# Windowed attention on Trainium2: the turn of the older chunk goes in front of the scores, its copy in front of the row maximum

## What is computed

```python
q, k = rmsnorm(rope(x @ wq.T)), rmsnorm(rope(x @ wk.T)); v = x @ wv.T
mask = (cols <= rows) & (rows - cols <= WINDOW)          # WINDOW = 128
scores = einsum('bqgtd,bqgsd->bqgts', q, k) / sqrt(64)   # 16 heads of q, one k
attn = softmax(where(mask, scores, NEG))
out = einsum('bqgts,bqgsd->bqgtd', attn, v)
return h + reshape(out) @ wo.T
```

## Time and profile before

| | |
|---|---|
| median of 3 timed runs | 976.79 us (975.57, 976.79, 984.98) |
| the profiled execution | 969.34 us, of which the span is 967.1 us |
| busy over the span: PE, DVE, ACT, POOL | 747.3, 630.0, 443.2, 383.2 us |
| mean granted TensorE clock | 0.897 of full speed |
| the four `windowed` stages, from the first to the last row maximum of each | 97.3 to 166.6, 227.6 to 296.6, 360.1 to 429.4 and 490.3 to 558.2 us |

### The profile page before, as it was taken

The page is one execution under the profiler, slowest core; times in us unless marked ns, Lnnn a source line. Parts: engine busy times, 40 slices in busy tenths (PEclk is TensorE's granted clock), DMA queues, the critical chain, the costliest instruction groups (busy, mean ns, idle before and its releaser), DMA issues. The chain is left out here.

```text
span 967.1 us, 21086 instructions
## 1 busy us (share of the span) xinstructions
PE 747.3 (77%) x8204; PEld 482.5 (50%) x8204; DVE 630.0 (65%) x1210; ACT 443.2 (46%) x1389; POOL 383.2 (40%) x432
## 2 busy tenths in 40 slices
PE   5577999887998879998769989978899965302870
PEld 5232677434775326774257744864577732201650
DVE  0378788596886787876968847676677728500890
ACT  0022899234995228991369935213666610200210
POOL 0035466254663445662646622652000000074475
PEclk9999999998999889999979999988999977655875
DMA  8144000080000620000300000008000021014200
GB/s 287 59 174 83 2 3 2 21 238 2 3 2 1 210 49 1 4 2 1 84 2 3 2 2 1 2 1 111 2 2 2 2 78 43 1 52 102 50 20 13
DMA packets 59992, 41.60 MB, mean 43 GB/s; under 512 B 51744, under 2 KB 57340, under 8 KB 59108
## 3 DMA queue, kind: packets, MB, share of 16 engines
q1 hardware_dynamic: 57446, 33.03, 13.7%
q10 hardware_dynamic: 144, 4.19, 1.1%
q0 software_dynamic: 2304, 3.04, 1.0%
HBM read 25.44 MB, written 7.15 MB: 34 GB/s over the span
## 5 line engine op out<-in xcount | busy, mean ns | idle before, releaser
L770 ACT ACTIVATE work<-ps,small,rq 128x160 f32<-128x160 f32 x512 | 243.1, 487 | 54.2 <-DVE small L719 53.7
L749 POOL TENSOR_TENSOR work<-work,small 128x512 f32<-128x512 f32 x128 | 133.3, 1042 | 138.1 <-DVE small L733 138.1
L716 DVE TENSOR_REDUCE ps<-ps 128x4 f32<-128x640 f32 x128 | 106.5, 832 | 52.4 <-PE ps L639 52.1
L727 DVE COPY pT<-ps 128x640 f32<-128x640 f32 x128 | 105.4, 823 | 8.2 <-PE ps L652 7.9
L770 ACT ACTIVATION_READ_ACCUMULATOR work<-ps,small,rq 128x1 f32 x512 | 105.2, 206 | 0.0
L1441 POOL DMA_INDIRECT sent_rows<-big,xb x32 | 30.9, 966 | 182.4 <-DVEq L1393 173.0
L639 PE MATMUL ps<-kT,big 64*128 64x160 f32 x1024 | 102.6, 322 | 0.0
L269 PE MATMUL ps<-xT,s_proj_w 64*128 64x512 f32 x288 | 78.9, 661 | 21.5 <-DVE prod L581 13.2
L669 PE MATMUL ps<-pT,vwin 128*64 128x128 f32 x1024 | 84.2, 282 | 10.6 <-ACT big L758 2.4
L609 POOL TENSOR_TENSOR big<-prod 128x1024 f32<-128x1024 f32 x28 | 66.4, 2372 | 47.5 <-DVE prod L581 47.0
L639 PEld LDWEIGHTS ps<-kT,big 64*128 64x128 f32 x1024 | 80.3, 200 | 0.4
(11 more groups left out here) (275 smaller groups left out, 1361.2 us busy)
## 6 DMA issues: line engine op xcount, KB each, us to landing
xb<-in_x SPq DMA_DIRECT2D x3, 4096.0 KB, 12.7
xb<-in_x ACTq DMA_DIRECT2D x1, 4096.0 KB, 15.1
vrem<-hl SPq DMA_DIRECT2D x64, 64.0 KB, 2.2
sent_rows<-empty_row SPq DMA_DIRECT2D x8, 325.0 KB, 10.0
s_proj_w<-in_proj_w SPq DMA_DIRECT2D x1, 1536.0 KB, 6.5
big<-sent_rows SPq DMA_DIRECT2D x5, 264.0 KB, 5.1
big<-sent_rows SPq DMA_DIRECT2D x5, 256.0 KB, 4.6
xb<-in_ffn_w SPq DMA_DIRECT2D x1, 1028.0 KB, 4.9
```

Source lines behind the costliest of these rows:

```text
L716: ch.step(v.tensor_reduce(row_max(c), ps[:, s_banks(c), 0:2 * SPAN].rearrange("p e (h k) -> p e h k", h=2), X, ALU.max))
L727: v.tensor_copy(pT[:, c % 2, :].rearrange("p (q r t) -> p r q t", r=2, t=D), ps[:, 4:6, 0:(NQ + 1) * D].rearrange("p r (q t) -> p r q t", ...
L749: g.tensor_tensor(probs[:, c % 3, :, 0:P], probs[:, c % 3, :, 0:P], bc(small[:, c % 4, 3, :], P), ALU.mult)
L770: nc.scalar.activation(probs[:, c % 3, q, :], bank[2 * (c % 2) + e][:, SPAN * hh:SPAN * hh + SPAN], ACT.Exp, bias=small[:, c % 4, 1, q:q + ...
```

## The change

PE's loop body in `windowed` calls `turn(n - 3)` first and not between `scores(n)` and `values(n - 4)`. DVE's loop body does the copy of the turned rows (now in a small function, `keep_turned_rows`) ahead of the row maximum of chunk n and not behind its bias. The waits of each step are the same as before.

```diff
--- before.py
+++ after.py
@@ -671,6 +671,8 @@
                     ins.then_inc(S["pv_done"], 1)
 
                 for n in range(CHUNKS + 4):
+                    if 3 <= n < CHUNKS + 3:
+                        turn(n - 3)
                     if n < CHUNKS:
                         scores(n)
                     if n == 1 and b + 1 < IMAGES:
@@ -682,8 +684,6 @@
                         turn_halves(tokensT, 6, S["tokens_turned"])
                     if n == 4 and b + 1 < IMAGES:
                         pe.wait_ge(S["h_ready"], 1)
-                    if 3 <= n < CHUNKS + 3:
-                        turn(n - 3)
                     if n >= 4:
                         values(n - 4)
                 pe.wait_ge(S["oT_ready"], CHUNKS)
@@ -701,6 +701,14 @@
             @block.vector
             def _(v):
                 ch = Chain(v, S["dve_chain"])
+
+                def keep_turned_rows(c):
+                    v.wait_ge(S["transposed"], c + 1)
+                    if c >= 2:
+                        v.wait_ge(S["pv_done"], c - 1)
+                    v.tensor_copy(pT[:, c % 2, :].rearrange("p (q r t) -> p r q t", r=2, t=D),
+                                  ps[:, 4:6, 0:(NQ + 1) * D].rearrange("p r (q t) -> p r q t", t=D)).then_inc(
+                                      S["pT_ready"], 1)
 
                 for n in range(CHUNKS + 3):
                     c = n
@@ -711,6 +719,8 @@
                         v.wait_ge(S["tokens_turned"], 1)
                         v.tensor_copy(h_next.rearrange("p (w j) d -> p j w d", w=2),
                                       bank[6][:].rearrange("p (j w d) -> p j w d", w=2, d=D)).then_inc(S["h_ready"], 1)
+                    if n >= 3:
+                        keep_turned_rows(n - 3)
                     if c < CHUNKS:
                         v.wait_ge(S["scores_done"], c + 1)
                         ch.step(v.tensor_reduce(row_max(c),
@@ -719,14 +729,6 @@
                         v.scalar_tensor_tensor(out=small[:, c % 4, 1, :].rearrange("p (e h) -> p e h", e=2),
                                                in0=row_max(c), scalar=-1.0, in1=rq[:, c], op0=ALU.mult,
                                                op1=ALU.mult).then_inc(S["bias_ready"], 1)
-                    c = n - 3
-                    if c >= 0:
-                        v.wait_ge(S["transposed"], c + 1)
-                        if c >= 2:
-                            v.wait_ge(S["pv_done"], c - 1)
-                        v.tensor_copy(pT[:, c % 2, :].rearrange("p (q r t) -> p r q t", r=2, t=D),
-                                      ps[:, 4:6, 0:(NQ + 1) * D].rearrange("p r (q t) -> p r q t", t=D)).then_inc(
-                                          S["pT_ready"], 1)
                     c = n - 1
                     if 0 <= c < CHUNKS:
                         v.wait_ge(S["exp_done"], NQ * (c + 1))
```

## The result

The changed kernel takes 995.62 us (median of four runs, 993.63 to 996.94), the kernel before 976.18 (974.29 to 984.98): 1.0185 times as long, with a 95% interval of 1.0143 to 1.0228. On a second occasion, with more runs of both, it was 1.0202 (1.0161 to 1.0244). The profiled execution of the changed kernel took 993.63 us with a span of 991.8.

The account below looks back on a forecast made before the run. A closed chain of waits through ACT's output copy was taken as the bound, 2.19 us a chunk rising to 2.40. At 6.0 us an image, 24 in all, 969.3 became 993.3, scaled to the median 1001 us; range 991 to 1011.

Parts of the forecast that it names:

- The closed chain through O: In the windowed loop, PE's values matmuls wait for ACT's output copy; this chain grows from 4.38 to 4.80 us per two chunks.
- T costs nothing between S and V, and lengthens the way from V to S: PE's turn fills a wait, free, between scores and values; ahead of scores it delays them 0.33 to 0.46 us.
- C in front of R: DVE's copy of turned rows, ahead of the row maximum, mostly hidden by scores; maximum starts 1.31 us after the turn.
- The overlap of 0.08 at the end of a DVE copy: On DVE, the row maximum starts 0.74 us after the turned-rows copy starts, though that copy's row lasts 0.82.
- The sum over the images: Windowed stages: 27 periods of 0.21 us, 5.7, plus 0.3 at the start: 6.0 us an image, 24 for four.
- the start-up: First chunks of each image: DVE's copy for chunk 0 precedes chunk 3's maximum, costing 0 to 0.74 us, taken as 0.3.
- The step to the median: Whole kernel: profiled 969.3 plus 24 gives 993.3 us; scaled by the timed median's 0.77% excess over the profiled run, 1001.
- The signs: Expected in the changed profile: maxima 2.40 us apart, PE idle 0.3 to 0.5 before values, ACT idle 0.25 a chunk.
- (1) *Faster: Values' wait for ACT's copy is coincidence; DVE's copy before the turn binds, also 4.38 us: 965, or 972 median-scaled; 4%.
- (2) *No difference: The turn runs early in PE's idle time before scores, so the chain does not grow: 975 to 979 us; 4%.
- (3) *Lower clock: PE's waits before values lower its granted clock, adding about 0.7 us a chunk, 75 in all: 1076 us; 3%.
- (4): On both changed engines, execution order is not the program's, so the change doesn't do what it says; excluded beforehand.

## Why the prediction was right, and where it was off

**The closed chain through O: right.** The forecast was 4.80 us for two chunks, the trace gives 4.79; a period of 2.40 was forecast and measured. Each link is within 0.01 of what was taken: T to C 0.57, C to R 0.74, R to B 0.86 for 0.87, V to its second part 0.62, and to T 0.38. The kernels with O moved show it as a cause: later by one exponential adds 0.23 a chunk in either order, earlier by one takes 0.23 away in the changed one.

**T costs nothing between S and V, and lengthens the way from V to S: right.** V starts 0.11 behind the end of O with T in front of it and without. Between V and S it costs 0.30 (from V's second part to S it is 0.68 to 0.69 where it was 0.38). It becomes a bound between S and V only once O is out of the way: V then starts 0.49 behind T.

**C in front of R: right.** Nearly hidden by S: S starts 0.30 behind T (0.33 to 0.46 was said), and the copy holds R until 1.31. Where R waits for S alone, in the kernel with PE's half, it starts 1.25 behind T (286.29 to 287.54): S to R is 0.95 there and not the 0.89 that I took from the kernel before. So the tie was resolved the way I took it, and the copy costs 0.06 of the 0.42 on two chunks; the other 0.36 are T in front of S. The forecast also said that this half is needed for the other, without a price; the kernel with PE's half alone gives it, 3.13 instead of 2.40.

**The overlap of 0.08 at the end of a DVE copy: right.** R starts 0.74 behind C although C's row lasts 0.82, at 287.27 and again at 289.43. By the Trainium skill, page "VectorE: DVE Perf Modes", section "The DRAIN you can't avoid", the next op does not start until the pipe empties; that rule by itself is not borne out here. The same paragraph adds that a next op that is not held starts earlier, and a start 0.08 before the end of the row agrees with that.

**The sum over the images: 24 us forecast, 21.1 measured in the loop.** Two small terms were mis-sized. I counted 27 longer periods an image where the maxima of chunks 5 to 31 have 26, and took 0.3 us for the start-up. Measured it is nothing: from the first maximum to the sixth 12.5, 11.5, 12.4 and 10.9 us, against 12.3, 12.1, 12.3 and 10.7. That PE's idle time there took in the copy is likely, but not shown. 4 x 26 x 0.206 is 21.4. The drain was put at zero, and the trace agrees: the three stretches from the last maximum of an image to the first of the next, with the drain in them, are 185.4 us together before and 185.7 after.

**The step to the median: right to 2 us.** The forecast was 1001, 5.4 us above the measured 995.6. Of these, 2.9 come from the sum above (24 for 21.1) and 0.6 from the median of the kernel before, which was 976.79 for three executions and is 976.18 with a fourth. Scaling by 976.79 / 969.34 put in only 0.2, since 976.79 + 24 is 1000.8. The last 1.7 is left between 976.2 + 21.1 = 997.3 and 995.6; the four executions of the changed kernel alone lie 3.3 apart.

**The signs.** Maxima 2.40 apart, T 0.38 behind V's second part, V 0.11 behind O, DVE idle in front of C (0.54 and 0.31) and not in front of R: as said. PE's idle time in front of V was put at 0.3 to 0.5 in each period; it is 0.22 and 0.70 in turn. The view puts the first of these down to "issue" and the second to the wrong copy. ACT's was put at 0.25 a chunk; 2.95 us of 40, at 2.40 a chunk, are 0.18.

**The rivals.** (1) *Faster*, because C in front of T binds: refuted, since the change took C from behind R and B and the loop got slower, and since O moved later in the kernel before adds 23.6 us with C untouched. The prediction let this chain close with the same 4.38. That sum holds time that V owed to its wait for O: T to V 0.61 and V to its second part 0.62, where they are 0.49 and 0.59 without that wait. The chain measures 4.22 where it binds. So it exists, with 0.16 of slack in the kernel before. (2) *No difference*: refuted. (3) *Lower clock*: the granted clock is 1.00 over 120 to 160, the 2.4 GHz level, although PE stands idle for up to 0.70 at a time; the loads of S last 0.57 to 0.58 as before. (4) was excluded by the order.

## What to carry to other kernels

Where three engines are busy for over 80% of a loop, look for the closed chain of waits and count over how many iterations it closes; a step that fills a wait is free (T between S and V), and the same step between the end of a wait and what the chain needs next counts (0.30 between V and S). An order changed on one engine is to be read together with the orders on the others: PE's half of this change alone cost 119 us, DVE's half 59, both together 19, and moving one copy on a third engine by one place turned 19 lost into nothing, and without the change gained 9, of which 5 are in the loop. A chain that closes with the right sum need not be the one that binds: its sum can contain a wait for another (here C's 4.38, of which 4.22 were its own). Before moving big steps around a single buffer, try to move its reader (here O) earlier, and check what the reader itself waits for.

## What was not expected of the hardware

In the kernel with O one exponential earlier, an exponential's row lasts 0.52 us where the kernel before has 0.48 to 0.49, and O's 0.41 instead of 0.38, while the starts stay 0.46 to 0.48 apart (285.05 and 285.53, for instance). The rows got longer and the work did not: ACT's rate is to be taken from the starts. Why they got longer is open; nothing here separates it. In the kernel before, the gap of 0.17 in front of S with ACT named behind it looked like the wait for the exponentials. But 0.17 also stands between V and its second part and between that part and T, where the view of the changed kernel names no wait and the row height changes, and there is no gap in the changed kernel where S follows T, both of 64 rows. With the wait really in front of S the same view shows 0.23 to 0.24.
